# Maxima's row transfers from ACT's queue, setup work moved ahead, last adapter batch in halves

## The chip, the cores and the metric

The kernel runs on one core of one Trainium2 chip. The metric is the device time of one execution in microseconds. Five engines run their own instruction streams: TensorE (PE, with its weight loads as PEld), VectorE (DVE), ScalarE (ACT), GpSimd (POOL) and SyncE (SP). They wait for each other through semaphores. Transfers are issued by an engine (rows named SPq or ACTq) and run on the core's DMA engines.

## The reference

x is 4 x 512 x 256 (batches, tokens, features), float32. Four layers follow one another, each conditioned by a row per batch:

```
L0: x += g1 * (softmax(q k^T) v @ Wo + bo),  q, k, v from mod(ln(x)) @ W + b,  16 heads of 16
    x += g2 * (gelu(mod(ln(x)) @ W1 + b1) @ W2 + b2),  hidden 1024
L1: x += ga * (a state-space layer with 64 complex states over mod(ln(x)))
    x += gf * (gelu_tanh(mod(ln(x)) @ W1 + b1) @ W2 + b2)
L2: as L0, with rotary embedding of q and k and without most biases
L3: y = gelu(x @ a1 @ b1, rank 8) @ a2 @ b2,  a and b made from the condition row per batch
    out = x + y
```

## The kernel before

**Engine streams.** Each engine's program is written out: setup, attention 0 (`att0`), MLP 0, MLP 1 with the state-space layer, attention 1 (`att1`), MLP 2 with the low-rank adapter (`low`), and the adapter of the last batch at the very end. Everything on one engine runs in the written order.

**Attention.** A table, `attention_schedule`, gives every task a step number; each engine walks through the steps and does its own kinds of tasks. 16 steps make one group G of four heads of one batch, so there are 16 groups and 256 steps. Tasks with a step below LEAD = -34 are the lead, done before the loop. In a step n TensorE makes one score tile (line 636, one of 512 wide), one product for the running maxima (L645, 32 steps ahead; DVE reduces pairs of them in L819), and every fourth step the product with V (L666, PV). ACT takes the exponential of each score tile (L723) and, at step 16G+20, copies the group's result out (kind O, L684), after a wait for the last PV. ACT also copies T, Q and K (L694, L703, L706) out of PSUM.

**Banks.** The score tiles and the Q, K, V, T, M and PJ results rotate through three PSUM banks (7, 0, 1) in the order in which TensorE makes them. `open` makes TensorE wait until the former user of the bank has been read.

**Row maxima.** At step 16G-13 TensorE turns the maxima (M, L609), DVE negates them into a high and a low part (L780, L781), and at step 16G-12 the task MROW sends them as two extra rows of Q into the tiles of group G: four transfers within SBUF (L911), 4 KB each. At step 16G TensorE waits for them (`mset`). MROW is SP's task.

**Stores and fills.** q and k are split into a high and a low part (kinds SQ, SK), stored to DRAM (WQ, WK; `save_parts`, L883, three transfers each) and loaded again in another layout (FILL; `fill`, L893, four transfers per group). For batch 0 of att0 the order on SP is: stores of half 0, fill of group 0, stores of the second quarter, fill of group 1, stores of half 1, fills of groups 2 and 3, stores of batch 1, MROW of group 0. WK of half 0 alone is issued by ACT. TensorE waits for the fill of group g 32 steps before its first score tile.

**DVE in the start.** Statistics of batch 2 (LNS, L390, L397, L399) come at steps -24 to -12, and at step -12 DVE copies the turned modulation columns (`setup_turned_dve`) that TensorE turned at step -20 (`mod_turn`).

**The end.** For batch 3 the adapter runs alone: DVE adds the MLP's result to x (L1119, L1123), TensorE turns x (L430), DVE copies (L1541), down (L1547), copy (L1555), up (L1562), ACT's gelu (L1570), down (L1575), copy (L1583), up (L1590), DVE adds (L1597), SP stores (L1602).

Of the kernel before, what the change touches and what calls it, by code (L numbers as in the profile page):

```python
# [23 lines left out]
P = 128  # L24
B, T, D = 4, 512, 256
TT = T // P
# [36 lines left out]
def attention_schedule(rope):  # L63
# [6 lines left out]
    for b in range(B):  # L70
        o = 64 * (b - 1)
        first = b == 0
        for t in range(TT):
            put((-100, -84)[b] if b < 2 else o - 88 + 4 * t, "LNS", b, t)
        put((-99, -72)[b] if b < 2 else o - 75, "LNN", b, 0)
        for i in range(2):
            put((-90, -36)[b] + i if b < 2 else o - 65 + 2 * i, "T", b, i)
        for half in range(2):
            for k, c in enumerate("QK"):
# [7 lines left out]
                put((-67, -59)[half] if first else at + 14, "W" + c, b, half)  # L87
# [76 lines left out]
def build(nc, A, out):  # L164
    scheds = [attention_schedule(False), attention_schedule(True)]

    with ExitStack() as ctx:
# [336 lines left out]
        class Attention:  # L504
# [114 lines left out]
            def pe(self, pe):  # L619
# [3 lines left out]
                for n in self.steps(self.pe_task(pe)):  # L623
                    if n == LEAD and self.a:
                        pe.wait_ge(mlp1.acc_free, B)
                    elif n == -20 and self.a == 0:
                        mod_turn(pe, 2, 3, 6)
# [43 lines left out]
            def act_task(self, act):  # L671
                def task(kind, b, i):
                    if kind == "LNN" and self.a and b < 2:
                        norm_apply(act, "a1", b)
                    if self.a == 0 and (b, i) == (0, 0):
                        if kind == "WK":
                            self.save_parts(act, kind, b, i)
# [130 lines left out]
            def dve(self, v, link):  # L808
                for n in self.steps(self.dve_task(v, link)):
                    if n == -12 and self.a == 0:  # L810
# [84 lines left out]

            def sync_task(self, sp):
                def task(kind, b, i):
                    if kind in ("WQ", "WK"):
                        if kind == "WQ" or b or i or self.a:
# [6 lines left out]
                    elif kind == "MROW":  # L906
                        g = b % 4
                        self.wait_read(sp, "M", b, 0)
                        for r in range(2):
                            for c in range(2):  # L910
                                sp.dma_start(QD[g // 2][64 * r + SROWS + c:64 * r + SROWS + c + 1,  # L911
                                                        2 * (g % 2):2 * (g % 2) + 2, :].rearrange(
                                                            "p j (q c) -> p (j q) c", c=P),
                                             mneg_d[b % 2][8 - 8 * r:16 - 8 * r, c, :]).then_inc(self.mset[g], 16)
# [587 lines left out]
        class Low:  # L1502
# [95 lines left out]

            def sync(self, sp):
                for b in range(B):  # L1600
                    sp.wait_ge(f_oo, b + 1)
                    sp.dma_start(out[b].rearrange("(t p) d -> p t d", p=P), batch(b)).then_inc(out_done, 16)  # L1602
                sp.wait_ge(out_done, 16 * B)
# [377 lines left out]
        def mlp2_dve(v, link):  # L1981
# [27 lines left out]
            mlp2.dve_acc(v, 3)  # L2009
            low.dve_turned(v, 3)  # L2010
            low.dve_down(v, 3)
            low.dve_down2(v, 3)
            low.dve_out(v, 3)
# [4 lines left out]
        def _(pe):  # L2018
# [41 lines left out]
            pe.wait_ge(f_oo, 3)  # L2060
            low.turn(pe, 3)
            low.down(pe, 3)
            low.up(pe, 3)
            low.down2(pe, 3)
# [253 lines left out]
```

## Time and profile before

| | |
|---|---|
| three timed runs | 991.09 median, 979.3 to 994.69 us |
| profiled execution | 983.21 us, span 981.4 us |
| mean granted TensorE clock | 0.966 |
| busy: PE, DVE, ACT, POOL | 903.0, 586.9, 520.2, 417.5 us |
| att0, from its first exponential to its last O copy | 75.0 to 298.8 us |
| att1, the same | 617.6 to 842.4 us |

The span is the time from the first to the last instruction of one execution on the core. Busy times overlap between engines. A granted clock of 1.00 is TensorE's full speed, 0.50 half of it.

### The profile page before, as it was taken

To read this page: it belongs to the slowest core of one execution; us is meant where nothing else is said; L and a number is where in the kernel's file an instruction comes from. 1 tells how busy PE (TensorE), PEld (TensorE's weight loads), DVE (VectorE), ACT (ScalarE), POOL (GpSimd) and SP (SyncE) were. 2 spreads that over 40 slices of the span, in tenths; PEclk is the share of its full clock that TensorE was granted. 3 is DMA by queue.
4 is the path that set the end of the run, shared out by engine and by line. 5 is a ranking of instruction groups with operands and counts; after the bars stand their busy time and mean duration, and the time that the engine had idled before them with its cause. 6 is when DMAs were issued, how large, how long until landed. Compare 5 with 4: busy or idle time off the path is not lost.

```text
span 981.4 us, 14537 instructions
## 1 busy us (share of the span) xinstructions
PE 903.0 (92%) x5232; PEld 540.5 (55%) x5232; DVE 586.9 (60%) x911; ACT 520.2 (53%) x950; POOL 417.5 (43%) x556
## 2 busy tenths in 40 slices
PE   5769999899999889998999998899999999999995
PEld 3334444334336778786877774343443433687772
DVE  4565877688975375564433288478778884234223
ACT  2116777476766444345364432467677777644430
POOL 4241142242657545438545326462541116664330
PEclk9887999899999999999999999799999999999996
DMA  7366645545310230114114137365464421100001
GB/s 218 113 176 190 219 144 155 178 131 163 91 45 28 80 126 1 33 45 156 65 64 159 12 96 181 117 193 154 127 212 126 109 79 47 34 13 1 22 23 43
DMA packets 67135, 102.33 MB, mean 104 GB/s; under 512 B 16524, under 2 KB 27864, under 8 KB 66680
## 3 DMA queue, kind: packets, MB, share of 16 engines
q1 hardware_dynamic: 64804, 99.10, 33.5%
q10 hardware_dynamic: 2260, 2.30, 0.9%
q8 instruction: 42, 0.69, 0.3%
q14 instruction: 29, 0.24, 0.1%
HBM read 64.65 MB, written 36.07 MB: 103 GB/s over the span
## 4 chain that ended last, share of the span: by engine, by line
PE 70%; DVE 8%; DMA 5%; issue 5%; ACT 4%; SPq 4%; POOL 4%; ACTq 0%; DVEq 0%; POOLq 0%
PE PS L1042 11%; PE PS L666 11%; PE PS L636 11%; PE PS L1024 11%; PE PS L593 6%; PE PS L584 5%; PE PS L645 3%; ACT PH L723 2%; DMA d_parts<-UR 2%; PE PS L430 2%; DMA UR<-UR 2%; DVE U L819 2%; PE PS L604 2%; SPq L883 2%; PE PS L1157 1%
## 5 line engine op out<-in xcount | busy, mean ns | idle before, releaser
L819 DVE TENSOR_REDUCE U<-PS 128x2 f32<-128x1024 f32 x256 | 308.8, 1220 | 87.0 <-PE PS L645 85.8
L723 ACT ACTIVATE PH<-PS 128x512 f32<-128x512 f32 x512 | 277.6, 598 | 113.3 <-PE PS L636 110.0
L636 PE MATMUL PS<-UR 50*128 50x512 f32 x512 | 198.3, 458 | 23.2 <-DMA UR<-UR 15.1
L645 PE MATMUL PS<-UR 48*128 48x512 f32 x512 | 195.0, 475 | 14.1 <-DVE U L819 8.7
L636 PEld LDWEIGHTS PS<-UR 50*128 50x128 f32 x512 | 83.1, 188 | 180.0 <-ACT PH L723 105.3
L1089 POOL TENSOR_TENSOR PHR<-PH,PHR 128x512 fp32r<-128x512 f32 x96 | 128.8, 1347 | 119.7 <-ACT PHR L1079 119.7
L1042 PE MATMUL PS<-UR,PHR 128*128 128x256 f32 x768 | 158.7, 290 | 4.9 <-POOL PHR L1089 3.8
L666 PE MATMUL PS<-PH,U 128*32 128x512 f32 x1024 | 137.3, 609 | 0.0
L1042 PEld LDWEIGHTS PS<-UR,PHR 128*128 128x128 f32 x768 | 124.5, 189 | 22.5 <-issue 15.5
L1042 PE MATMUL PS<-W2R,PHR 128*128 128x256 f32 x384 | 108.2, 282 | 0.0
L1078 ACT ACTIVATE PH<-PS,col 128x512 f32<-128x512 f32 x64 | 43.9, 686 | 99.9 <-PE PS L1024 99.9
L645 PEld LDWEIGHTS PS<-UR 48*128 48x128 f32 x512 | 78.0, 189 | 31.2 <-DVE U L819 14.6
L1024 PE MATMUL PS<-UR 128*128 128x512 f32 x192 | 78.8, 411 | 4.7 <-issue 2.1
L584 PE MATMUL PS<-XN,WA 128*128 128x256 f32 x256 | 75.3, 428 | 2.2 <-ACT XN L694 2.2
L1024 PE MATMUL PS<-UR,W1R 128*128 128x512 f32 x192 | 76.7, 399 | 0.0
L1024 PE MATMUL PS<-XNR,UR 128*128 128x512 f32 x192 | 76.4, 398 | 0.0
L1042 PEld LDWEIGHTS PS<-W2R,PHR 128*128 128x128 f32 x384 | 72.3, 188 | 2.9 <-issue 1.2
L861 POOL TENSOR_TENSOR x<-x,tsc 128x256 f32<-128x256 f32 x32 | 23.5, 733 | 98.9 <-DVE tsc L792 98.2
L584 PEld LDWEIGHTS PS<-XN,WA 128*128 128x128 f32 x256 | 49.3, 207 | 22.9 <-issue 12.2
L404 POOL TENSOR_TENSOR rs<-ve,mhalf 128x4 f32<-128x4 f32 x24 | 25.2, 1051 | 76.9 <-DVE ve L399 76.7
L850 POOL TENSOR_TENSOR U<-U 128x512 f32<-128x512 f32 x16 | 20.4, 1277 | 65.6 <-issue 34.3
L1078 ACT ACTIVATE PH<-PS 128x512 f32<-128x512 f32 x32 | 19.1, 596 | 53.2 <-PE PS L1024 53.2
(221 smaller groups left out, 1251.9 us busy)
## 6 DMA issues: line engine op xcount, KB each, us to landing
UR<-d_parts SPq DMA_DIRECT2D x128, 192.0 KB, 4.1
d_parts<-UR SPq DMA_DIRECT2D x84, 256.0 KB
d_o<-U SPq DMA_DIRECT2D x32, 256.0 KB, 2.3
U<-in_L_cond_W_dram SPq DMA_DIRECT2D x8, 1024.0 KB, 7.7
W<-in_L_cond_W_dram SPq DMA_DIRECT2D x24, 256.0 KB, 3.0
U<-d_o SPq DMA_DIRECT2D x32, 128.0 KB
U<-d_rec SPq DMA_DIRECT2D x16, 256.0 KB
gates<-d_gate SPq DMA_DIRECT2D x3, 1024.0 KB, 5.2
```

What stands on the lines that cost most here:

```text
L404: link(pool.tensor_tensor(rs[:, 0, :], ve[:, :], mhalf[:, :], ALU.pow))
L584: ins = pe.matmul(dst[:, 0:D], WA[:, "QK".index(kind), k, h * P:(h + 1) * P], XN[:, b % 2, k, c], start=(k == 0), stop=(k == 1))
L593: ins = pe.matmul(dst[:, 0:D], src[:, k, i * P:(i + 1) * P], w[:, k, :], start=(k == 0), stop=(k == 1))
L636: self.close(pe.matmul(dst, KP[g // 2][r:r + SROWS + 2, j, kt * P:(kt + 1) * P], QP[g // 2][r:r + SROWS + 2, j, :], start=True, stop=True) ...
L645: ins = pe.matmul(bank(2 + (w + 2) % 4), QP[g // 2][r:r + SROWS, j, qt * P:(qt + 1) * P], KP[g // 2][r:r + SROWS, j, :], start=True, stop= ...
L666: ins = pe.matmul(PS[32 * j:32 * j + 32, 6, :], Vt[b % 2][:, kt, 4 * g + j, :], PH[:, m % 2, j, :], start=(kt == 0), stop=(kt == 3))
L723: nc.scalar.activation(PH[:, m % 2, j, :], self.where("ST", n), ACT.Exp).then_inc(self.a_free, 1)
L819: v.tensor_reduce(mx[:, G % 2, :].rearrange("p (r c) -> p r c", r=2)[:, :, c // 2], PS[:, 2 + (w + 1) % 4:4 + (w + 1) % 4, :], AX.X, ALU.m ...
L1024: ins = pe.matmul(bank(4 + q % 2), w[:, k, c], a[:, b % 2, k, :], start=(k == 0 and i == 0), stop=(k == 1 and i == 2))
L1042: ins = pe.matmul(self.acc(b, t), a[:, q % 4, c], w[:, m, :], start=(m == 0 and i == 0 and t % 2 == 0), stop=(m == FM - 1 and i == 2 and s ...
L1078: nc.scalar.activation(PH[:, 0, q % 4, :], bank(4 + q % 2), self.func, bias=bias)
L1089: pool.tensor_tensor(PHR[:, 0, q % 4, :], PH[:, 0, q % 4, :], HH[:, q % 4, :].bitcast(F32), ALU.subtract).then_inc(self.h_low, 1)
```

## The change

1. MROW of all groups of both attentions is ACT's task: `maxima(act, b)` waits for DVE's M result and issues the same four transfers from ACT's queue. SP issues none of them.
2. In att0, the stores of half 1 of batch 0 are issued by ACT at step -34, after group 0's fill has landed; SP keeps WQ of half 0 and the second quarter.
3. In att0, the statistics and the normalization of batch 2 are in the lead (steps -55 and -54); the evacuation of the modulation rows (`setup_more_dve`) is done ahead of the task FILL 2 in place of WQ 1; the turn and its columns come at the first step of the loop.
4. The adapter of batch 3 runs in halves of two token tiles, each with its own banks, copies and store; ACT and not DVE copies the turned x, and TensorE does two matmuls without use ahead of it.

```diff
--- before.py
+++ after.py
@@ -71,8 +71,8 @@
         o = 64 * (b - 1)
         first = b == 0
         for t in range(TT):
-            put((-100, -84)[b] if b < 2 else o - 88 + 4 * t, "LNS", b, t)
-        put((-99, -72)[b] if b < 2 else o - 75, "LNN", b, 0)
+            put((-100, -84)[b] if b < 2 else -55 if b == 2 and not rope else o - 88 + 4 * t, "LNS", b, t)
+        put((-99, -72)[b] if b < 2 else -54 if b == 2 and not rope else o - 75, "LNN", b, 0)
         for i in range(2):
             put((-90, -36)[b] + i if b < 2 else o - 65 + 2 * i, "T", b, i)
         for half in range(2):
@@ -84,7 +84,7 @@
                 if rope:
                     put(at + (1 if first else 5), "R" + c, b, half)
                 put(at + (2 if first else 7 if rope else 4), "S" + c, b, half)
-                put((-67, -59)[half] if first else at + 14, "W" + c, b, half)
+                put((-67, -59 if rope else -34)[half] if first else at + 14, "W" + c, b, half)
         for g in range(4):
             put((-62, -60, -57, -56)[g] if first else o + 17 + 16 * g, "FILL", b, g)
         for t in range(TT):
@@ -623,7 +623,7 @@
                 for n in self.steps(self.pe_task(pe)):
                     if n == LEAD and self.a:
                         pe.wait_ge(mlp1.acc_free, B)
-                    elif n == -20 and self.a == 0:
+                    elif n == LEAD:
                         mod_turn(pe, 2, 3, 6)
                     if n == 0:
                         pe.wait_ge(self.init, 1)
@@ -672,9 +672,13 @@
                 def task(kind, b, i):
                     if kind == "LNN" and self.a and b < 2:
                         norm_apply(act, "a1", b)
-                    if self.a == 0 and (b, i) == (0, 0):
-                        if kind == "WK":
-                            self.save_parts(act, kind, b, i)
+                    if kind == "WK" and self.a == 0 and b == 0:
+                        if i == 1:
+                            act.wait_ge(self.filled[0], FILLS)
+                            self.save_parts(act, "WQ", b, i)
+                        self.save_parts(act, kind, b, i)
+                    elif kind == "MROW":
+                        self.maxima(act, b)
                     if not self.on_act(kind) and kind != "O":
                         return
                     if kind == "O":
@@ -807,7 +811,7 @@
 
             def dve(self, v, link):
                 for n in self.steps(self.dve_task(v, link)):
-                    if n == -12 and self.a == 0:
+                    if n == LEAD and self.a == 0:
                         setup_turned_dve(v, link)
                     w = n + LOOK
                     if 0 <= w < NSTEP and w % 2:
@@ -893,25 +897,25 @@
                         sp.dma_start(dst[64 * r:64 * r + SROWS, 2 * (g % 2):2 * (g % 2) + 2, :],
                                      src[:, 4 * (g % 2) + r:4 * (g % 2) + 4:2, :]).then_inc(self.filled[g], 16)
 
+            def maxima(self, eng, G):
+                g = G % 4
+                self.wait_read(eng, "M", G, 0)
+                for r in range(2):
+                    for c in range(2):
+                        eng.dma_start(QD[g // 2][64 * r + SROWS + c:64 * r + SROWS + c + 1,
+                                                 2 * (g % 2):2 * (g % 2) + 2, :].rearrange("p j (q c) -> p (j q) c", c=P),
+                                      mneg_d[G % 2][8 - 8 * r:16 - 8 * r, c, :]).then_inc(self.mset[g], 16)
+
             def sync_task(self, sp):
                 def task(kind, b, i):
                     if kind in ("WQ", "WK"):
-                        if kind == "WQ" or b or i or self.a:
+                        if b or self.a or (kind, i) == ("WQ", 0):
                             self.save_parts(sp, kind, b, i)
                     elif kind == "FILL":
                         if (b, i) == (0, 1):
                             self.save_parts(sp, "WQ", 0, 0, 1)
                             self.save_parts(sp, "WK", 0, 0, 1)
                         self.fill(sp, b, i)
-                    elif kind == "MROW":
-                        g = b % 4
-                        self.wait_read(sp, "M", b, 0)
-                        for r in range(2):
-                            for c in range(2):
-                                sp.dma_start(QD[g // 2][64 * r + SROWS + c:64 * r + SROWS + c + 1,
-                                                        2 * (g % 2):2 * (g % 2) + 2, :].rearrange(
-                                                            "p j (q c) -> p (j q) c", c=P),
-                                             mneg_d[b % 2][8 - 8 * r:16 - 8 * r, c, :]).then_inc(self.mset[g], 16)
                     elif kind == "LDW":
                         if self.a and b == 0:
                             sp.wait_ge(mlp1.w2, FM * B)
@@ -1596,11 +1600,105 @@
                 xs = batch(b).rearrange("p (c a) d -> p a c d", a=2)
                 v.tensor_tensor(xs, xs, PS[:, 6:8, :].rearrange("p a (c d) -> p a c d", d=D), ALU.add).then_inc(f_oo, 1)
 
+            def last_pe(self, pe):
+
+                def half(c):
+                    return slice(D * c, D * (c + 1))
+
...
+                pe.wait_ge(f_oo, 3)
+                pe.wait_ge(mlp2.acc_free, B - 1)
+                for _ in range(2):
+                    pe.matmul(bank(5), WA[:, 0, 0, 0:P], WA[:, 1].rearrange("p k n -> p (k n)"), start=True, stop=True)
+                turn_half(0)
+                turn_half(1)
+                down_(0)
+                up_(0)
+                down_(1)
+                down2_(0)
+                up_(1)
+                up2_(0)
+                down2_(1)
+                up2_(1)
+
+            def last_act(self, act):
+                for c in range(2):
+                    act.wait_ge(f_t, 2 * B - 1 + c)
+                    nc.scalar.activation(xT[1][:, :, D * c:D * (c + 1)], bank(6 + c).rearrange("p (k n) -> p k n", k=DH),
+                                         ACT.Copy).then_inc(f_yo, 1)
+                for c in range(2):
+                    act.wait_ge(f_y, 2 * B - 1 + c)
+                    nc.scalar.activation(gT[1][:, :, D * c:D * (c + 1)], PS[:, 2 * c:2 * c + 2, 0:D],
+                                         ACT.Gelu).then_inc(f_yo, 1)
+
+            def last_dve(self, v):
+                b = B - 1
+                v.wait_ge(mlp2.w2, FM * B)
+                for c in range(2):
+                    v.tensor_tensor(tsc[:, 2 * c:2 * c + 2, :], bank(2 + c).rearrange("p (t d) -> p t d", d=D),
+                                    gates[:, 0, 1, b:b + 1, :].to_broadcast([P, 2, D]), ALU.mult).then_inc(mlp2.acc_free, 1)
+                    v.wait_ge(mlp2.acc_free, B + c)
+                    xs = x[:, TT * b + 2 * c:TT * b + 2 * c + 2, :]
+                    v.tensor_tensor(xs, xs, tsc[:, 2 * c:2 * c + 2, :], ALU.add).then_inc(mlp2.xd, 1)
+                for c in range(2):
+                    v.wait_ge(f_z, B + c)
+                    v.tensor_copy(z1[1][:, D * c:D * (c + 1)], bank(4 + c, D)).then_inc(f_zo, 1)
+                for c in range(2):
+                    v.wait_ge(f_z2, B + c)
+                    v.tensor_copy(z2[1][:, D * c:D * (c + 1)], bank(4 + c, D)).then_inc(f_z2o, 1)
+                for c in range(2):
+                    v.wait_ge(f_o, B + c)
+                    v.wait_ge(mlp2.xd, B + c)
+                    xs = x[:, TT * b + 2 * c:TT * b + 2 * c + 2, :]
+                    v.tensor_tensor(xs, xs, PS[:, 6 - 6 * c:8 - 6 * c, 0:D], ALU.add).then_inc(f_oo, 1)
+
             def sync(self, sp):
-                for b in range(B):
+                for b in range(B - 1):
                     sp.wait_ge(f_oo, b + 1)
                     sp.dma_start(out[b].rearrange("(t p) d -> p t d", p=P), batch(b)).then_inc(out_done, 16)
-                sp.wait_ge(out_done, 16 * B)
+                for c in range(2):
+                    sp.wait_ge(f_oo, B + c)
+                    t = slice(2 * c, 2 * c + 2)
+                    sp.dma_start(out[B - 1].rearrange("(t p) d -> p t d", p=P)[:, t, :],
+                                 batch(B - 1)[:, t, :]).then_inc(out_done, 16)
+                sp.wait_ge(out_done, 16 * (B + 1))
 
 
         att0, att1 = Attention(0, 6), None
@@ -2006,11 +2104,7 @@
             low.dve_down(v, 2)
             low.dve_down2(v, 2)
             low.dve_out(v, 2)
-            mlp2.dve_acc(v, 3)
-            low.dve_turned(v, 3)
-            low.dve_down(v, 3)
-            low.dve_down2(v, 3)
-            low.dve_out(v, 3)
+            low.last_dve(v)
 
         block = ctx.enter_context(nc.Block())
 
@@ -2057,12 +2151,7 @@
                     mlp2.product1(pe, q + 2)
                 mlp2_pe(pe, q)
                 mlp2.product2(pe, q)
-            pe.wait_ge(f_oo, 3)
-            low.turn(pe, 3)
-            low.down(pe, 3)
-            low.up(pe, 3)
-            low.down2(pe, 3)
-            low.up2(pe, 3)
+            low.last_pe(pe)
 
         @block.scalar
         def _(act):
@@ -2115,7 +2204,7 @@
                 if q < 3:
                     mlp2.act_w2(act, q + 1)
             low.act_gelu(act, 2)
-            low.act_gelu(act, 3)
+            low.last_act(act)
 
         @block.vector
         def _(v):
@@ -2134,7 +2223,7 @@
             v.tensor_copy(czero2[:, :], czero[:, :]).then_inc(mods_set, 1)
             setup_columns(v, link)
             for t in lead[turned_:]:
-                if t == ("WQ", 0, 1):
+                if t == ("FILL", 0, 2):
                     setup_more_dve(v, link)
                 att0.dve_task(v, link)(*t)
             att0.dve(v, link)
```

Left out above are the helpers of `last_pe`: each does one piece of `low` (turn, down, up, down2, up2) for 256 of the 512 tokens, waiting for its own half's copy.

## Rows read from the trace of the kernel before

**Rows 1.** The page, busy time of each engine.

```profile
PE 903.0 (92%) x5232; PEld 540.5 (55%) x5232; DVE 586.9 (60%) x911; ACT 520.2 (53%) x950; POOL 417.5 (43%) x556
```

**Rows 2.** Timeline of all engines, 107 to 126: start, us, engine, line, what.

```profile
109.90 3.74 SPq L911 DMA_DIRECT2D UR<-UR  x4
...
110.79 0.60 ACT L684 ACTIVATE U<-PS 128x512 f32<-128x512 f32 x1 [0.43 <-PE PS L666]
...
111.29 1.08 ACT L723 ACTIVATE PH<-PS 128x512 f32<-128x512 f32 x2
...
112.38 0.50 PE L636 MATMUL PS<-UR 50*128 50x512 f32 x1
...
125.21 0.50 PE L636 MATMUL PS<-UR 50*128 50x512 f32 x1 [0.17 <-ACT PH L723]
```

**Rows 3.** Line 911 alone: ns min/median/max of one issue.

```profile
L911 SPq DMA_DIRECT2D UR<-UR x128: 620/656/1797, 66.3 to 819.3; - x128
```

**Rows 4.** Timeline of ACT, 0 to 31.

```profile
3.12 0.21 ACT L1355 ACTIVATE csig<-col 128x8 f32<-128x8 f32 x1 [0.17 <-DVE col L1367]
3.13 0.37 ACTq L2074 DMA_DIRECT2D WA<-in_L_cond_Wq_dram  x1
3.54 0.49 ACTq L2074 DMA_DIRECT2D WA<-in_L_cond_Wk_dram  x1
...
24.80 3.25 ACTq L883 DMA_DIRECT2D d_parts<-UR  x3
28.09 0.84 ACT L703 ACTIVATE U<-PS,col 128x256 f32<-128x256 f32 x2 [3.49 <-issue]
```

**Rows 5.** Timeline of SP, around 354, the later load of the same kind.

```profile
354.42 0.47 SPq L2236 DMA_DIRECT2D WA<-in_L_cond_Wk_dram  x1
```

**Rows 6.** Timeline of PE, instructions after long idle times (in brackets).

```profile
60.39 0.50 PE L645 MATMUL PS<-UR 48*128 48x512 f32 x2 [2.48 <-DVE U L819]
...
74.23 0.76 PE L636 MATMUL PS<-UR 50*128 50x512 f32 x1 [6.56 <-DMA UR<-UR]
...
179.79 0.50 PE L636 MATMUL PS<-UR 50*128 50x512 f32 x1 [3.61 <-DMA UR<-UR]
...
300.25 0.74 PE L1024 MATMUL PS<-UR 128*128 128x512 f32 x1 [2.08 <-issue]
...
331.77 0.39 PE L1042 MATMUL PS<-UR,PHR 128*128 128x256 f32 x1 [2.50 <-POOL PHR L1089]
...
476.37 0.50 PE L1024 MATMUL PS<-UR 128*128 128x512 f32 x1 [1.94 <-DVE XNR L1111]
...
616.80 0.76 PE L636 MATMUL PS<-UR 50*128 50x512 f32 x1 [4.99 <-DMA UR<-UR]
```

**Rows 7.** Busy time by stretch; the granted clock stands before DMA share and GB/s.

```profile
61.30:64.70 3.40, 3.40 (x11) 2.21 (x10) 1.96 (x3) 0.47 (x1) 3.31 (x4) 0.51 0.90 197
75.00:84.80 9.80, 9.56 (x28) 5.09 (x27) 4.14 (x5) 5.28 (x10) 0.34 (x1) 0.50 0.69 238
300.70:303.60 2.90, 2.90 (x8) 2.23 (x7) 1.51 (x8) 0.44 (x1) 1.56 (x2) 0.50 0.10 23
332.00:335.00 3.00, 3.00 (x20) 2.60 (x20) 0.00 (x0) 0.66 (x2) 2.59 (x8) 1.00 0.26 72
477.90:481.10 3.20, 3.20 (x12) 2.79 (x11) 1.34 (x8) 1.26 (x2) 1.75 (x6) 0.50 0.00 0
...
965.00:969.00 4.00, 2.40 (x11) 0.57 (x12) 1.46 (x3) 0.00 (x0) 0.00 (x0) 0.50 0.00 0
```

**Rows 8.** Timeline of all engines, the end: the turn and the last store.

```profile
963.16 1.94 PE L430 MATMUL PS<-ident,x 128*128 128x128 f32 x8 [2.67 <-DVE x L1123]
...
978.06 0.37 SPq L1602 DMA_DIRECT2D out_dram<-x  x1
```

**Rows 9.** Timelines of DVE and SP, the first maxima.

```profile
55.25 0.28 DVE L781 SCALAR_TENSOR_TENSOR UR<-PS,UR 16x128 fp32r<-16x128 f32 x1
...
66.28 3.20 SPq L911 DMA_DIRECT2D UR<-UR  x4
```

More of the change, by code:

```diff
@@ L1597, in dve_out, with turn_half, down_half, down_ @@
                 v.tensor_tensor(xs, xs, PS[:, 6:8, :].rearrange("p a (c d) -> p a c d", d=D), ALU.add).then_inc(f_oo, 1)
+            def last_pe(self, pe):
+                def half(c):
+                    return slice(D * c, D * (c + 1))
+                def turn_half(c):
+                    pe.wait_ge(mlp2.xd, B + c)
+                    for k in range(DH):
+                        for t in range(2):
+                            ins = pe.transpose(PS[:, 6 + c, D * k + P * t:D * k + P * (t + 1)],
+                                               x[:, TT * (B - 1) + 2 * c + t, k * P:(k + 1) * P], ident[:, :])
+                    ins.then_inc(f_t, 1)
+                def down_half(j, src, c):
+                    for g in range(4):
+                        ins = pe.matmul(PS[32 * g:32 * g + 32, 4 + c, 0:D], wide[:, j, B - 1, g % 2, :],
+                                        src[1][:, g % 2, half(c)], start=True, stop=True)
+                    return ins
+                def down_(c):
+                    pe.wait_ge(f_yo, 2 * B - 1 + c)
+                    down_half(0, xT, c).then_inc(f_z, 1)
+                def up_(c):
+                    pe.wait_ge(f_zo, B + c)
+                    for h in range(DH):
+                        r = slice(64 * h, 64 * h + 64)
+                        ins = pe.matmul(bank(2 * c + h, D), btr[r, 0, B - 1, h * P:(h + 1) * P], z1[1][r, half(c)],
+                                        start=True, stop=True)
+                    ins.then_inc(f_y, 1)
+                def down2_(c):
+                    pe.wait_ge(f_yo, 2 * B + 1 + c)
+                    down_half(2, gT, c).then_inc(f_z2, 1)
+                def up2_(c):
+                    pe.wait_ge(f_z2o, B + c)
+                    for t in range(2):
+                        r = slice(64 * t, 64 * t + 64)
+                        ins = pe.matmul(bank(6 - 6 * c + t, D), z2[1][r, (2 * c + t) * P:(2 * c + t + 1) * P],
+                                        btr[r, 1, B - 1, :], start=True, stop=True)
+                    ins.then_inc(f_o, 1)
+                pe.wait_ge(f_oo, 3)
[12 more added lines that the diff above has]
+                up2_(1)
```

## The prediction

> **What bounds the kernel now.** I read the page first. TensorE is busy for 92% of the span and ACT for 53% [rows 1], so the kernel is a TensorE stream with some holes, and a change pays either by closing a hole or by opening one. Then I listed every TensorE idle time above 0.9 us. Four of these holes lie where the change works [rows 6]: 2.48 us ended by a DVE reduction at 60.39, and 6.56 us at 74.23, 3.61 us at 179.79 and 4.99 us at 616.80, these three ended by the maxima's row transfers (UR<-UR). After the longest the granted clock is 0.50, the 1.2 GHz level, from 75 to 84.8 [rows 7].
>
> Why the first of these row transfers is late is seen in two rows: its data were ready at 55.53, when DVE ended L781, but SP issued it at 66.28 [rows 9], because SP goes through its tasks in order and fills and stores stood ahead of it.
>
> The steady loop of one group, 16 steps, comes next (223.8 us of att0's table entry over 16 groups are 14.0), since 30 of 32 of the moved tasks fall into it. In the timeline of a group with a V product every fourth step [rows 2] the reader should see how little ACT runs behind TensorE: ACT's O copy starts at 110.79, the exponentials of steps 4 and 5 follow at 111.29, in 1.08 us, and TensorE's L636 of step 6, which needs the first of them, starts at 112.38. Score tiles, V, Q, K and M share three PSUM banks, so a score product waits for the exponential of its third predecessor in the rotation. Where no such product lies between, ACT is the last to come: TensorE's L636 at 125.21 waits 0.17 us for it [rows 2]. ACT has 47% idle time over the span, but in lumps of some half microsecond; it has none of several microseconds that TensorE doesn't feel.
>
> **The change, part by part.**
>
> *The maxima's transfers on ACT's queue.* One issue costs SP 656 ns at the median and 620 at the least [rows 3]; four come to 4 x 0.656 + 3 x 0.04 = 2.74 us. The trace has no such transfer on ACT, so its cost there is bounded. The nearest pair is the same load of a 256 KB weight: 0.37 (Wq) and 0.49 us (Wk) on ACT [rows 4], 0.47 (Wk) on SP [rows 5]. An issue costs the same on both, and I take 2.74 us. The low end is 4 x 0.37 + 0.12 = 1.6 us, as for that cheapest load on ACT; the high end is the stores on ACT, 3.25 us for three [rows 4], or 4.3 for four.
>
> Does ACT compute meanwhile? After the three stores at 24.80 the next activation starts at 28.09, and its idle time of 3.49 us is put down to issue [rows 4]. So the issue holds ACT up. But the activation ahead overlaps: L2074 starts at 3.13, 0.01 us after the activation ahead of it [rows 4]. At a group's MROW (step 4) the instruction ahead is the O copy of an earlier group. The M result is there by then (SP issued at 109.90 [rows 2], before the O copy at 110.79), so the added wait itself costs nothing. The four issues run from 110.80 to 113.54. Queued behind them are the exponentials of steps 4 to 7 and the Q or K copies, and TensorE waits for those. Step 4's exponential would start at 113.54 and not at 111.29, 2.25 us later. The following L636 has at most 112.38 less 111.83 (111.29 + 0.54), or 0.55 us, of slack, some of it the semaphore's way; I take 0.35 to 0.45. That leaves a hole of 1.8 us in groups with a product every fourth step, and 2.2 us where ACT already is the last to come. ACT then catches up within the next steps, but TensorE, the bound, doesn't. Mean 2.0 us. G = 0 of either attention has no exponentials behind it, so 2 x 15 = 30 groups pay: **+60 us**, with ends of 30 x 0.9 = 27 and 30 x 3.6 = 108 (a hole is the issue time less some 0.7 us, so 1.6 less 0.7 and 4.3 less 0.7).
>
> The Trainium skill speaks against this edit (DMA: Bandwidth & Descriptors, section "Issuing engines are not separate DMA queues"): transfers begun from several engines run on the same DMA engines, and only the sequencer's time for the issue is saved, "usually small relative to the DMA itself". Here that issue time is the whole matter, and it moves from SP, which waits for others most of the time, to the engine nearest to the bound. By that page alone the sum would stay near nought.
>
> *The clock.* A hole has a second price. Of the holes between 1.9 and 2.5 us [rows 6], those at 60.39 (2.48), 300.25 (2.08) and 476.37 (1.94) were followed by a stretch at 0.50, the one at 331.77 (2.50) was not [rows 7]; eight shorter ones (1.0 to 1.6 us, not shown) were not either. Such a stretch is 2.9 to 3.4 us long [rows 7] and costs half of that, 1.7 us. The new holes are at the lower edge of this: from none to 3 in 4 of 30 may drop the clock. I take 12: **+20 us**, ends 0 and 23 x 1.7 = 39.
>
> *The three waits for the row transfers.* ACT is free when M is ready for G = 0, so the transfer goes at 55.5 and not at 66.3 [rows 9]. It took 74.23 less 69.48 (66.28 + 3.20), 4.75 us, from the last issue to TensorE's start, so it lands near 63, and TensorE reaches step 0 at 67.67 less the 4 us of the next part, near 64. The wait of 6.56 us goes, and with it the 9.8 us at half clock behind it, of which I count 4.0 us as won and the rest as latency. What is late next are the fills of group 2. They need the half-1 stores, which leave ACT as soon as group 0's fill has landed and no longer SP after group 1's fill; they land earlier, so the fills do too. ACT has hardly other work there, and three banks cover its Q copies if they come some 4 us later. If these six stores crowd the quarter-1 stores beside them, group 1's fill could be 1 to 2 us late. Attention 1: 4.99 us and 3.3 us for its slow stretch (some 7 us). G = 6 of attention 0: 3.61 us and, by the same share, 2.4. Sum **-10.6 - 8.3 - 6.0 = -25 us**.
>
> *Statistics of batch 2, modulation turn and columns into the lead.* DVE and TensorE wait there for group 0's fill, so they are covered. This takes away what stood before 60.39: 2.48 us and the slow stretch behind it, 1.7 [rows 7]: **-4 us**. PE's four transposes fall before group 0's fill, at no cost.
>
> *The last batch's adapter in halves.* Now the chain from the turn at 963.16 to the last store's issue at 978.06 [rows 8] is 14.9 us of nine dependent pieces, at clock 0.50 (965 to 969 [rows 7]). In halves, the residual of half 0 is ready 1.2 us earlier, and half 0's pieces run under half 1's. TensorE's ten half pieces take 1.0 us each at clock 0.50 (a whole turn took 1.94) and 0.5 at full clock, and DVE's and ACT's copies 0.4 to 0.7 each. Placed one behind the other in the new order, the last issue comes at 970.6 if the two added matmuls keep the clock up, and at 974.4 if not: 4 to 8 us less, taken as **-6 us**.
>
> *SP without MROW* and the moved gate loads change nothing: nobody waits for SP after these edits.
>
> **The sum.** -25 - 4 - 6 = -35, +60 + 20 = +80, net +45 us. The profiled execution took 983.2 us (span 981.4), 8 us less than the median of the three timed runs, 991.1, which lie between 979.3 and 994.7. I count from 987, the mean of the two: **1032 us**.
>
> **Rivals.**
> *The issues are hidden (ends on the other side).* Place: ACT's queue at step 4 of each group. If the sequencer got to the four issues while earlier exponentials are still queued in the engine, only a part would delay step 4's. Against it: L2074 had no wait of its own, yet went only at 3.13, with the activation ahead (3.12) that had waited for DVE [rows 4]; so an issue doesn't pass a waiting instruction. It decides from 35 / 30 = 1.2 us of hole per group, that is issues of 1.9 us in all. Fully hidden: 987 - 35 = 952. Half hidden (a hole of 1.0 us, no clock drops): 952 + 30 = 982. The Trainium skill gives ScalarE an instruction queue 8 deep in strict order (TensorE: Matmul & The Clock Gate, "Architectural detail: the array is 16× 32×32, not 1× 128×128"); by that rule it would be the fully hidden case, and the row at 3.13 speaks against it.
> *The holes come, the clock holds.* For: none of the eight shorter holes dropped it. 952 + 60 = 1012.
> *The clock drops after nearly every hole.* For: three of four did. 952 + 60 + 51 = 1063.
> *The start doesn't shorten as told.* The half-1 stores on ACT crowd the fills and the start keeps its 15 us: 1032 + 15 = 1047.
>
> **How the numbers follow.** Forecast (holes, some drops; 1015 to 1048) 0.42; clock holds 0.20; drops nearly always 0.10; start kept 0.11; half hidden 0.11; fully hidden 0.06. 8 in 10 go from 1000 to 1063: that leaves out both hidden cases (0.17) and a bit at the top. A measurement of this kernel can tell about 2%, 20 us, from no change. Faster than 971: 0.06. Within 971 to 1011: half hidden and a third of the case at 1012, 0.18. Slower: 0.76.
>
> **What would show it.** ACTq rows for the maxima of 0.62 to 0.70 us each beside ACT's O copy; after them TensorE holes of 1.8 to 2.2 us, ended by ACT's L723 line; O copies 16 us apart where they were 14.0; TensorE's mean clock below 0.966 and stretches of 0.50 in the attentions. No wait for UR<-UR at step 0. The forecast is wrong if ACT's issues take under 0.4 us, or if O copies stay 14 us apart.

## The result, and the profile after

The changed kernel takes **1097.9 us** at the median of four runs (1093.2 to 1099.6), the one before 985.9: a ratio of 1.115, with an interval of 1.105 to 1.125. It is 112 us slower, where +45 was forecast. The profiled executions span 1097.1 us and 981.4 us. Where the runs of one kernel fell into a fast state and a slow one, over 1.5% longer (experiments 2, 4, 8 and 12), the median given is that of the fast ones alone.

From the page of the kernel after: its busy times, the granted clock by slices, the chain, and the costliest group of TensorE. The line numbers have moved by a few: L636 is still the score product, the exponential is L727, the O copy L688, the row transfers L905.

```profile
PE 974.3 (89%) x5256; PEld 560.7 (51%) x5256; DVE 588.3 (54%) x914; ACT 522.0 (48%) x952; POOL 416.3 (38%) x556
...
PEclk9788888887889999999999997897979688799999
...
PE 71%; ACT 7%; ACTq 7%; DVE 5%; issue 4%; POOL 3%; DMA 3%; SPq 1%; DVEq 0%; POOLq 0%
...
L636 PE MATMUL PS<-UR 50*128 50x512 f32 x512 | 229.8, 526 | 74.8 <-ACT PH L727 73.4
```

Against [rows 1], DVE, ACT and POOL are busy for nearly the same time. TensorE, with 24 matmuls more, is busy for 71 us more. Work didn't grow: the same 512 score products take 526 ns each, where they took 458 before, and TensorE stood idle ahead of them for 73.4 us, waiting for exponentials (L727). On the chain of work that ended last, ACT's transfer issues (ACTq) have 7% of the span, where they had none. The clock's digits (tenths of full speed in 40 slices) show where TensorE was slower: mostly 8 in attention 0, 6 to 9 in attention 1, 9 between and behind them. So two things are to be told apart, idle time and slower matmuls.

I cut both executions at the first and the last score product of each attention. The windows (columns: stretch, its length, busy time of PE, PEld, DVE, ACT, POOL, granted clock, DMA share, GB/s) of the kernel before:

```profile
0.00:74.23 74.23, 48.58 (x168) 28.23 (x168) 40.49 (x92) 12.63 (x23) 29.81 (x47) 0.91 0.57 168
74.23:296.10 221.87, 210.55 (x1205) 87.79 (x1206) 172.41 (x237) 154.00 (x289) 81.14 (x155) 0.96 0.49 146
296.10:616.80 320.70, 297.64 (x1739) 235.75 (x1738) 165.50 (x312) 141.69 (x241) 167.62 (x210) 0.99 0.26 82
616.80:839.70 222.90, 216.20 (x1225) 89.01 (x1228) 161.61 (x194) 158.34 (x301) 78.91 (x82) 0.98 0.44 127
839.70:981.40 141.70, 130.03 (x906) 99.74 (x904) 46.85 (x78) 53.53 (x98) 59.99 (x64) 0.93 0.06 21
```

and of the kernel after:

```profile
0.00:71.38 71.38, 52.74 (x169) 30.92 (x169) 39.11 (x91) 11.87 (x23) 27.35 (x46) 0.83 0.60 180
71.38:353.40 282.02, 238.98 (x1208) 94.86 (x1210) 174.76 (x239) 155.45 (x290) 82.77 (x157) 0.84 0.39 114
353.40:667.20 313.80, 295.98 (x1738) 234.45 (x1735) 164.17 (x310) 139.67 (x240) 163.64 (x207) 0.99 0.26 80
667.20:963.10 295.90, 258.60 (x1226) 101.12 (x1226) 163.99 (x195) 160.20 (x303) 82.45 (x86) 0.82 0.35 99
963.10:1097.10 134.00, 128.00 (x930) 99.38 (x928) 46.23 (x81) 54.85 (x100) 60.04 (x64) 1.00 0.07 22
```

By stage the change gives -2.8, **+60.1**, -6.9, **+73.0** and -7.7 us, together +115.7. The loss lies in the two loops of 16 groups; every other stage gained.

One group of the kernel after, in the timeline:

```profile
211.43 0.60 ACT L688 ACTIVATE U<-PS 128x512 f32<-128x512 f32 x1 [0.43 <-PE PS L666]
211.43 2.62 ACTq L905 DMA_DIRECT2D UR<-UR  x4
...
214.15 2.27 ACT L727 ACTIVATE PH<-PS 128x512 f32<-128x512 f32 x4 [2.13 <-DVE tsc L796]
...
214.80 0.50 PE L636 MATMUL PS<-UR 50*128 50x512 f32 x1 [1.71 <-ACT PH L727]
...
215.72 1.82 PE L666 MATMUL PS<-PH,U 128*32 128x512 f32 x8
...
220.68 1.07 PE L666 MATMUL PS<-PH,U 128*32 128x512 f32 x8
```

ACT spends 2.62 us on the four issues; the next exponential follows at 214.15 (the releaser named there, L796, is not what held it: ACT's own queue is). TensorE has used up its three banks and waits 1.71 us. The product behind it, L666 at 215.72, takes 1.82 us where its like at 220.68 takes 1.07: the clock has fallen (0.50 from 216 to 219) and comes back in between. The O copies of attention 0 are 17.3 us apart on average (15 intervals from 95.95 to 355.41). Measured the same way they were 13.4 apart before (96.77 to 298.23); the forecast put this at 14.0 before and 16 after. Slow stretches can be longer, as windows some groups later show:

```profile
252.00:263.00 11.00, 9.49 (x53) 3.40 (x45) 8.21 (x10) 5.45 (x11) 1.28 (x1) 0.93 0.46 110
264.60:273.40 8.80, 8.80 (x34) 3.07 (x32) 4.10 (x4) 2.82 (x6) 0.00 (x0) 0.50 0.34 134
276.00:283.00 7.00, 6.23 (x37) 2.57 (x29) 5.97 (x9) 3.41 (x7) 0.85 (x2) 1.00 0.62 151
285.00:293.00 8.00, 8.00 (x30) 2.57 (x28) 4.10 (x4) 2.94 (x6) 2.15 (x4) 0.50 0.14 51
```

The stretch from 264.6 to 273.4 is wholly at the 1.2 GHz level with TensorE busy all the time. Read so in steps of 1 us, the clock is at 0.5 in 26 stretches of the two loops, about 192 us in all or 7.4 each; in the loops of the kernel before it was in 3, 26 us in all. One of the 26 stands at the start of attention 1, as one did before; the other 25 follow 25 of the 29 holes of over 1.4 us that TensorE waited for exponentials. The four holes with no slow stretch behind them were 1.55, 1.72, 2.26 and 2.67 us long, and the shortest with one was 1.50, so length alone doesn't tell them apart.

### The profile page after: what moved, and what is told of

It reads as the page before. It is cut to its first block, busy times and chain, and to the rows that moved or that the text cites. A ratio compares the mean times of both kernels' runs of the same rounds, so it can differ in the third digit from the quotient of the medians.

```text
span 1097.1 us, 14588 instructions
## 1 busy us (share of the span) xinstructions
PE 974.3 (89%) x5256; PEld 560.7 (51%) x5256; DVE 588.3 (54%) x914; ACT 522.0 (48%) x952; POOL 416.3 (38%) x556
## 4 chain that ended last, share of the span: by engine, by line
PE 71%; ACT 7%; ACTq 7%; DVE 5%; issue 4%; POOL 3%; DMA 3%; SPq 1%; DVEq 0%; POOLq 0%
PE PS L666 14%; PE PS L636 13%; PE PS L1046 10%; PE PS L1028 9%; ACTq L905 6%; PE PS L593 6%; PE PS L584 5%; PE PS L645 4%; ACT PH L727 4%; PE PS L604 2%; PE PS L430 2%; DMA d_parts<-UR 2%; ACT U L688 2%; PE PS L1161 1%; PE PS L1149 1%
## 5 line engine op out<-in xcount | busy, mean ns | idle before, releaser
L727 ACT ACTIVATE PH<-PS 128x512 f32<-128x512 f32 x512 | 277.9, 598 | 228.5 <-PE PS L636 151.5
L636 PE MATMUL PS<-UR 50*128 50x512 f32 x512 | 229.8, 526 | 74.8 <-ACT PH L727 73.4
L636 PEld LDWEIGHTS PS<-UR 50*128 50x128 f32 x512 | 97.5, 217 | 274.3 <-ACT PH L727 162.9
L645 PE MATMUL PS<-UR 48*128 48x512 f32 x512 | 224.0, 537 | 9.3 <-DMA UR<-d_parts 6.5
L666 PE MATMUL PS<-PH,U 128*32 128x512 f32 x1024 | 166.9, 730 | 0.0
L645 PEld LDWEIGHTS PS<-UR 48*128 48x128 f32 x512 | 92.7, 218 | 23.4 <-issue 9.1
L584 PE MATMUL PS<-XN,WA 128*128 128x256 f32 x256 | 80.8, 452 | 4.2 <-ACT XN L698 4.2
L584 PEld LDWEIGHTS PS<-XN,WA 128*128 128x128 f32 x256 | 52.5, 221 | 27.4 <-issue 15.2
L593 PE MATMUL PS<-WA,XN 128*128 128x256 f32 x128 | 44.6, 480 | 1.1 <-ACT U L707 1.1
L666 PEld LDWEIGHTS PS<-PH,U 128*32 128x32 f32 x1024 | 21.5, 116 | 44.8 <-issue 16.7
```

Source lines behind the costliest of these rows:

```text
L584: ins = pe.matmul(dst[:, 0:D], WA[:, "QK".index(kind), k, h * P:(h + 1) * P], XN[:, b % 2, k, c], start=(k == 0), stop=(k == 1))
L593: ins = pe.matmul(dst[:, 0:D], src[:, k, i * P:(i + 1) * P], w[:, k, :], start=(k == 0), stop=(k == 1))
L636: self.close(pe.matmul(dst, KP[g // 2][r:r + SROWS + 2, j, kt * P:(kt + 1) * P], QP[g // 2][r:r + SROWS + 2, j, :], start=True, stop=True) ...
L645: ins = pe.matmul(bank(2 + (w + 2) % 4), QP[g // 2][r:r + SROWS, j, qt * P:(qt + 1) * P], KP[g // 2][r:r + SROWS, j, :], start=True, stop= ...
L666: ins = pe.matmul(PS[32 * j:32 * j + 32, 6, :], Vt[b % 2][:, kt, 4 * g + j, :], PH[:, m % 2, j, :], start=(kt == 0), stop=(kt == 3))
L727: nc.scalar.activation(PH[:, m % 2, j, :], self.where("ST", n), ACT.Exp).then_inc(self.a_free, 1)
```

## The experiments

Times are medians; the kernel before, timed beside each batch of experiments, was between 984.7 and 987.6. I held three theories. **A**: the issues on ACT open a hole in every group, and the clock falls after nearly each; both cost. **B**: the issues alone are the price and the clock is a symptom. **C**: another part of the change costs.

**1. All row transfers back on SP**, the rest kept.

```diff
 # act_task
-                    elif kind == "MROW":
-                        self.maxima(act, b)
 # sync_task
+                    elif kind == "MROW":
+                        self.maxima(sp, b)
```

> The changed kernel with the row transfers of the maxima on SP's queue in every group again; half-1 stores on ACT, statistics and the halved last adapter stay. Theory A (nearly the whole loss is the issue time on ACT and the TensorE clock that it costs): the 1097.9 us fall by the two loops' loss of 59.8 + 72.7 = 132 us, to about 965 to 985. Theory C (the stores on ACT, the statistics or the adapter cost a part): it stays 20 us or more above 985, over 1005.

Measured 970.7 us, ratio 0.984 (0.977 to 0.991; a ratio is to the kernel before). The windows of its two loops:

```profile
71.71:291.07 219.36, 208.49 (x1208) 86.31 (x1210) 173.66 (x239) 154.44 (x290) 82.88 (x157) 0.97 0.49 147
611.11:835.14 224.03, 216.11 (x1225) 89.04 (x1229) 161.80 (x194) 158.35 (x301) 78.94 (x82) 0.98 0.44 126
```

The loops are as long as before the change, to 3 us. The rest of the change is a small gain, and C falls.

**2. Only the row transfers moved**, in the kernel before (its MROW branch leaves `sync_task`; `act_task` calls `maxima(act, b)`).

> The kernel before with one part of the change alone: the row transfers of all 32 groups begun from ACT's queue. Theory A: it carries the whole loss, 985 + 112 to 132 less the some 15 us that the earlier first step of either attention gives: 1085 to 1110. Theory C: clearly less, under 1060. The forecast on record, with its holes of 2.0 us and 12 drops, would give 60 + 20 - 25 = +55, 1040.

Measured 1091.3 us, of two runs that lie apart (1083.4 and 1099.2), ratio 1.105 (1.091 to 1.119): this one part carries the whole loss, to within what these runs can tell. In the profile (1099.2 us) the loops are 277.8 and 295.7 us; the start is 6.0 us shorter, and the stretch between the attentions 6.7 us.

**3. On ACT for the first group of either attention alone.**

```diff
-                    elif kind == "MROW":
+                    elif kind == "MROW" and b == 0:
                         self.maxima(act, b)
 # sync_task
+                    elif kind == "MROW" and not (b == 0):
+                        self.maxima(sp, b)
```

> The changed kernel with the row transfers on ACT for the first group of either attention alone and on SP for the other 30. Theory A: no holes inside the loops, and both starts are shortened as they were: 965 to 975, under the run with all on SP by what the first wait for the rows costs (up to 10.6 and 8.3 us). Rival: SP's queue is free by then at either start since the half-1 stores left it, and this run and the one with all on SP agree within 3 us.

Measured 968.7 us, ratio 0.982 (0.975 to 0.989). Against experiment 1 that is 2 us, less than the two intervals can tell, so both the forecast and its rival stand by the time. The profiles show that each was right for one attention. The stretch between the attentions is 314.0 us against 320.0: ahead of attention 1, TensorE waited 4.62 us for the rows with all on SP, and doesn't here. In attention 0 neither kernel has such a wait at step 0, since SP's queue is free without the half-1 stores; start and loop together are 293.5 against 291.1, no gain.

**4. The holes filled.** The last S product ahead of the hole is repeated eight times into the same bank, before its signal; the result is the same.

```diff
-                        ins = pe.matmul(bank(2 + (w + 2) % 4), ...)
+                        for _ in range(9 if n % 16 == 5 else 1):
+                            ins = pe.matmul(bank(2 + (w + 2) % 4), ...)
```

(the dummy product of the last steps likewise)

> The changed kernel, its transfers on ACT in all groups, with 8 repeats of one 0.21 us S product on TensorE in the step ahead of each hole (1.7 us of matmuls that repeat a result), so that TensorE is busy while ACT issues. The exponentials wait as long as before. Theory A (hole and clock multiply): the clock stays at 1.0 in the loops, the slow stretches go (TensorE's busy time had grown by 28 us in the first loop and 42 us in the second), and the time falls by 40 to 70 us to 1030 to 1060. Theory B (the issues on ACT are the whole price, the clock is a symptom beside it): within 10 us of 1098.

Measured 1042.6 us, ratio 1.053 (1.044 to 1.062): 55.3 us less than the changed kernel, although TensorE does 288 matmuls more. Its timeline around one group, and the windows of its two loops:

```profile
214.41 2.62 ACTq L907 DMA_DIRECT2D UR<-UR  x4
...
214.85 1.98 PE L646 MATMUL PS<-UR 48*128 48x512 f32 x9
...
217.78 0.50 PE L636 MATMUL PS<-UR 50*128 50x512 f32 x1 [0.72 <-ACT PH L729]
...
218.21 1.06 PE L668 MATMUL PS<-PH,U 128*32 128x512 f32 x8
```

```profile
73.70:324.50 250.80, 236.77 (x1336) 108.98 (x1337) 175.29 (x239) 154.95 (x290) 83.55 (x158) 0.98 0.43 127
...
638.80:898.10 259.30, 246.17 (x1354) 111.57 (x1356) 164.50 (x195) 159.91 (x303) 82.77 (x86) 0.98 0.39 113
```

(L646 is the S product here, L668 PV.) ACT issues as long, 2.62 us, and releases TensorE as late; but TensorE has worked until 0.72 us before, the clock stays at 0.98, and L668 takes 1.06 us. B falls. This splits the price: filled holes against none (experiment 1) 71.9 us, idle against filled holes 55.3 us. By the profiles' loops it is 66.7 and 67.8 us. The 29 holes of the changed kernel sum to 69.3 us, so the first part is about what the holes alone explain. Read in steps of 1 us, the loops here are at 0.5 for about 20 us, against 192: a microsecond at half clock cost 0.3 to 0.4 us, not a half.

**5, 6 and 12. One, two and three of each group's four on ACT**, the others on SP. Both engines call `maxima`; `on_act` is true in ACT's call and false in SP's.

```diff
+                        if (2 * r + c < 1) == on_act:   # 2 in experiment 6, 3 in experiment 12
                             eng.dma_start(QD[g // 2][...], mneg_d[G % 2][...]).then_inc(self.mset[g], 16)
```

> The changed kernel with one of each group's four row transfers on ACT and three on SP, in all groups. Theory A (the burst on ACT opens a hole of its length less the half to one us that the score banks cover, 2.4 us for four issues of 2.6, and each such hole costs 1.8 us more by the clock): one issue of 0.65 us lies under the cover, no holes, no drops: 965 to 975, as with all on SP. Rival (every issue on ACT costs its length): 30 x 0.65 = 20 us more, 990.

> The changed kernel with two of each group's four row transfers on ACT and two on SP. Theory A: 1.3 us of issues less 0.5 to 1.0 of cover leave holes of 0.3 to 0.8 us in 30 groups, 9 to 24 us, too short for the clock to fall: 980 to 995. Rival (the clock already falls after short holes): 2 us each more, over 1020. By proportion of the whole loss of 127 us: 1034.

> The changed kernel with three of each group's four row transfers on ACT and one on SP. Two on ACT left holes of 1.07 us and the clock up, four left 1.7 to 2.4 and the clock down after nearly each. By length three leave 1.07 + 0.66 = 1.7 us: 30 x 1.7 = 51 us, 1022, if the clock stays up; with half of the drops 1045; with the clock down after each, at 1.9 us, 1078. Theory A takes 1040 to 1078; a price in proportion to the issues on ACT would be 970.7 + 3/4 x 127 = 1066 (two gave 17 of 127 where proportion had 64, so it is already unlikely).

Measured 968.5 us (ratio 0.980, 0.974 to 0.986), 987.4 us (1.000, 0.997 to 1.004) and 1038.4 us (1.053, 1.045 to 1.061). With the ends of the series, none and four, and with the granted clock, the median over the same runs:

| on ACT | us | over none | mean clock |
|---|---|---|---|
| 0 | 970.7 | | 0.971 |
| 1 | 968.5 | -2.2 | 0.975 |
| 2 | 987.4 | +16.7 | 0.976 |
| 3 | 1038.4 | +67.7 | 0.941 |
| 4 | 1097.9 | +127.2 | 0.900 |

A price per issue would be a straight line, and one of burst length alone a straight line behind the first. The step from two to three is 51 us, 30 x 0.66 = 20 of them by length, and it is there that the clock begins to fall. Three came out just under theory A's 1040 to 1078, nearest to its case of half of the drops (1045). Two fell into theory A's range, though with longer holes than its 0.3 to 0.8 us. Experiment 6 shows a hole, and the window around it:

```profile
122.57 0.49 PE L636 MATMUL PS<-UR 50*128 50x512 f32 x1 [1.08 <-ACT PH L727]
```

```profile
80.00:200.00 120.00, 111.05 (x648) 46.08 (x644) 89.56 (x106) 83.16 (x156) 39.72 (x62) 1.00 0.57 172
```

Eight holes of 0.38 to 1.27 us, each ended by an exponential, lie in these 120 us, and the mean clock is 1.00 over them. With three on ACT the holes of the first loop are 1.04 to 2.56 us (in the profile, an execution of 1048.4 us, longer than the median), with four 1.55 to 4.08.

**7. All four on ACT in every fourth group only** (`b % 4 == 2`, 8 groups in all).

> The changed kernel with all four row transfers on ACT in every fourth group only (groups 2, 6, 10, 14 of either attention, 8 in all) and on SP in the others: the price of a hole that stands alone. If each costs what 30 of them cost on average, (1097.9 - 970.7) / 30 = 4.2 us: 970.7 + 34 = 1005. If holes apart from each other cost what the forecast took, 2.0 us and 1.7 in 12 of 30 cases: 970.7 + 8 x 2.7 = 992. If the clock never falls after a lone one: 970.7 + 8 x 2.4 = 990.

Measured 1009.3 us, ratio 1.020 (1.013 to 1.027): 38.6 us over experiment 1, **4.8 us for each hole**. They need no neighbours to be dear. The eight are 2.28 to 4.21 us long, 2.7 at the mean, and seven of them are followed by a slow stretch; the shortest, at 665.41, isn't. Two of them, a stretch behind each, and two stretches away from any:

```profile
162.80 0.79 PE L636 MATMUL PS<-UR 50*128 50x512 f32 x1 [3.40 <-ACT PH L727]
...
276.29 0.79 PE L636 MATMUL PS<-UR 50*128 50x512 f32 x1 [2.42 <-ACT PH L727]
```

```profile
150.00:160.00 10.00, 9.40 (x57) 4.00 (x49) 7.66 (x9) 6.30 (x12) 2.31 (x2) 1.00 0.55 138
163.00:173.00 10.00, 10.00 (x36) 3.45 (x36) 3.68 (x3) 4.46 (x10) 2.31 (x2) 0.50 0.36 100
180.00:218.00 38.00, 36.87 (x223) 15.04 (x221) 32.16 (x39) 27.19 (x51) 15.45 (x44) 1.00 0.57 159
277.00:291.00 14.00, 13.99 (x59) 4.22 (x57) 6.50 (x7) 7.04 (x14) 8.17 (x12) 0.50 0.11 31
```

**8. All four on ACT in all groups, one at a time.**

```diff
-        put(16 * G - 12, "MROW", G, 0)
+        for i in range(4):
+            put(16 * G - (12, 10, 7, 5)[i], "MROW", G, i)
```

> The changed kernel with all four row transfers of every group on ACT, but begun one at a time, 12, 10, 7 and 5 steps ahead of the group's first score in place of all at 12. ACT issues as long in all (32 x 2.6 us) but never more than 0.65 us between two exponentials. Theory A (the burst is the price): the holes are gone, 965 to 980. Rival (ACT's total time is the price, as it is 70% busy in the loops and the copies of queries and keys fall in the same steps): a part of the 127 us stays, over 1000.

Measured 973.0 us, ratio 0.985 (0.977 to 0.993). It is all but experiment 1's time: 125 of the 127 us are gone, and the other 2 are less than these runs can tell. ACT still issues all 128 transfers, most in 0.63 us each, now between exponentials (L728):

```profile
207.66 0.63 ACTq L907 DMA_DIRECT2D UR<-UR  x1
208.38 0.60 ACT L728 ACTIVATE PH<-PS 128x512 f32<-128x512 f32 x1
208.44 0.63 ACTq L907 DMA_DIRECT2D UR<-UR  x1
208.88 1.57 ACT L728 ACTIVATE PH<-PS 128x512 f32<-128x512 f32 x3
```

It was the burst, not ACT's load. The schedule has a weak point: the last row goes out only five steps ahead, and in the trace it lands late now and then, at the worst by this:

```profile
102.21 0.79 PE L637 MATMUL PS<-UR 50*128 50x512 f32 x1 [2.37 <-DMA UR<-UR]
```

**9 to 11. The other parts**, each undone in the kernel of experiment 3: the half-1 stores on SP (`-34` to `-59`, the ACT branch for them out), the last adapter whole (the calls of `last_pe`, `last_act`, `last_dve` back to `low`'s), the statistics of batch 2 and the modulation turn and columns in their old steps.

> The kernel with rows on ACT for the first group alone (968.7 us), and its half-1 stores of the start begun from SP again, in their old places. Theory A (a burst of issues on ACT costs there too): six stores held ACT for 9.7 us at the start, and TensorE waited 2.1 us for the copies of queries and keys behind them; step 0 comes earlier than 70.3, by some 2 us, as in the kernel before with only the rows moved (68.3): 964 to 968. Rival (the forecast on record: the stores on ACT land earlier and shorten the start): 3 to 6 us later, 972 to 975.

> The kernel with rows on ACT for the first group alone (968.7 us), and the last adapter whole as before. The forecast on record gave the halves 6 us: 974.7; the tail should be 20.9 us long again against 14.1, with the TensorE clock at 0.5. Rival: the output's transfer hides it, within 2 us of 968.7.

> The kernel with rows on ACT for the first group alone (968.7 us), and the statistics of the third batch element, and the turn and columns of the modulation, in their old places inside the loops. The forecast on record gave their move 4 us: 972 to 973. Rival: they lie beside other work in either place, within 2 us, or they delay the start and cost it.

Measured 971.0, 976.6 and 970.0 us, ratios 0.985 (0.980 to 0.989), 0.990 (0.986 to 0.994) and 0.984 (0.978 to 0.990), against 968.7 and 0.982 of experiment 3. The adapter's halves give 7.9 us, and every run with the whole adapter is over every run of experiment 3 (971.2 at the least against 970.4 at the most); in the profile the part behind attention 1's last product is 141.1 us with the whole adapter and 134.0 with halves. The other two are under what these runs can tell. The stores are the more instructive: on SP, step 0 comes at 62.5 and not at 70.2, but the loop behind it is 235.4 us long and not 223.3. TensorE waits there for what SP then sends late:

```profile
65.11 0.49 PE L645 MATMUL PS<-UR 48*128 48x512 f32 x1 [2.21 <-DMA UR<-d_parts]
...
87.20 0.79 PE L636 MATMUL PS<-UR 50*128 50x512 f32 x1 [3.80 <-DMA UR<-UR]
```

So theory A's forecast for it (964 to 968) missed: the earlier start is real and given back. The statistics look alike in the profiles: with them in their old places step 0 comes at 77.2 and not at 70.2, and the loop is 218.2 us long and not 223.3.

## Why the prediction was too low

The direction was right, and so was the mechanism of the hole: ACT's issues open one in 29 groups of the forecast's 30, it is about 1.7 or 2.4 us long in most where 1.8 and 2.2 were forecast, and the O copies stand further apart. The sum failed by 67 us, most of it in one step.

- **The clock, +20: the step that failed.** "From none to 3 in 4 of 30 may drop the clock. I take 12", at 1.7 us each. It fell behind 25 of 29 holes, and the stretches were 7.4 us long, not 2.9 to 3.4. Experiment 4 puts the price at 55 to 68 us, over the stated end of 39. Three of four holes of such length had been followed by 0.50 [rows 7]; I discounted them by eight shorter ones, and took the length of the slow stretch from the two MLP stages and the start, though the one row of a loop, 75 to 84.8, was 9.8 us long [rows 7], and my own term for attention 1 counted a stretch of "some 7 us". The rival "drops nearly always" had the count nearly right, but at 1.7 us each it also stopped at 1063. Half of 7.4 us would have been too much in turn: by experiment 4 a drop cost some 2.1 to 2.7 us. Experiment 7 shows that density isn't the reason: a hole with three groups of none between it and the next costs 4.8 us, against 2.0 + 0.7 in the forecast. Why the clock fell behind some holes and not behind others, and what ended a slow stretch, stays open.
- **The holes, +60.** Mis-sized by 7 to 12 us: experiments 4 and 1 differ by 66.7 us in the loops and 71.9 at the medians. Fifteen holes of attention 0 sum to 37.8 us and fourteen of attention 1 to 31.5. Most of the excess sits in six groups with holes of 2.9 us and more, where the four issues took longer than 2.74 us. Two of them, the issues and the hole behind:

```profile
75.73 4.98 ACTq L905 DMA_DIRECT2D UR<-UR  x4
...
81.41 0.79 PE L636 MATMUL PS<-UR 50*128 50x512 f32 x1 [4.08 <-ACT PH L727]
...
171.71 4.61 ACTq L905 DMA_DIRECT2D UR<-UR  x4
...
177.07 0.79 PE L636 MATMUL PS<-UR 50*128 50x512 f32 x1 [3.71 <-ACT PH L727]
```

  The median issue on ACT is 0.63 us, 0.66 on SP, so "an issue costs the same on both" held, but the median hid the long ones, 1797 ns already on SP [rows 3] and up to 2626 ns on ACT. The end of 4.3 us held all but three of the bursts.
- **The three waits, -25.** Too large. Attention 1's gave 6 to 7 us (8.3 forecast; experiments 2 and 3). The start gave 6.0 with the rows alone and 2.8 in the changed kernel (10.6 forecast). ACT's six half-1 stores took 10.73 us on its queue and held back the copies of queries and keys, and group 1's fill came later; the rows of the kernel after:

```profile
39.17 10.73 ACTq L887 DMA_DIRECT2D d_parts<-UR  x6
...
50.53 2.07 PE L593 MATMUL PS<-WA,XN 128*128 128x256 f32 x4 [1.08 <-ACT U L707]
...
57.66 0.79 PE L645 MATMUL PS<-UR 48*128 48x512 f32 x2 [2.63 <-DMA UR<-d_parts]
```

  Three banks were to cover ACT's Q copies "if they come some 4 us later"; they came behind the whole 10.73 us of issues, and TensorE waited 1.08 us for them. That the stores there shorten the start was false: by experiment 9 they move a wait from the loop to the start. The wait of 3.6 us at group 6 did go, and it is still there (2.72 us) in experiment 1.
- **Statistics -4 and last adapter -6.** Measured 1.3 at the medians (3.2 in the profiles), not to be told from nought, and 7.9 (7.1 in the profile). The clock stayed up there, as hoped for:

```profile
1083.76 1.88 PE L1649 MATMUL PS<-WA 128*128 128x512 f32 x4
...
1093.65 1.27 SPq L1699 DMA_DIRECT2D out_dram<-x  x2
```

- **The base of 987** held (985.9). With what was measured the sum is: holes +67 to +72, clock +55 to +68, waits about -13 (2.8 + 6.9 + 3.6), statistics -1 to -3, adapter -7 to -8, or +98 to +119, around the measured +112.
- **The rivals.** The issues were not hidden, and the rows at 211.43 and 214.15 show how it goes: the first issue starts with the O copy and doesn't wait for its end, but the next exponential waits for all four. By the Trainium skill ScalarE has an instruction queue in strict order (TensorE: Matmul & The Clock Gate, "Architectural detail: the array is 16× 32×32, not 1× 128×128"). The trace agrees with the order, and it doesn't lead to the fully hidden case that the prediction drew from it: the queue let the issues begin early here, by the 0.60 us of the O copy, and no more. The Trainium skill calls the issue time "usually small relative to the DMA itself" (DMA: Bandwidth & Descriptors, "Issuing engines are not separate DMA queues"). For this change that doesn't carry over: bursts of 2.6 us and more on the engine that feeds the bound cost 4.2 us per group, holes and clock together, where the same issues on SP opened none of these holes.

## What to carry to other kernels

A queue's place is priced by the burst, not by its sum: 128 issues on ACT cost 127 us in bursts of four and, one at a time, no more than these runs can tell from nought. So spread issues over the steps, or leave them on the engine that is waited for least. Price a TensorE hole with its clock, by a slow stretch of the same stage, and take the drop as the rule once rows at that length show it in most cases. Where only one transfer of a class is late, try moving that one: the first group's alone took 6 us off the stretch ahead of attention 1 in the profile, though the whole gain of 2 us over all on SP isn't shown by the times.

## What the hardware showed beyond that

- A slow stretch can go on while TensorE is busy all the time: 8.8 us at 0.50 with 8.80 us of busy time, and 14 us after a 2.42 us hole in experiment 7. At 0.5 the loop's exponentials come every 3.1 us per two steps (267.33, 270.48, 273.50 in the kernel after), at full clock every 1.7 us (275.45, 277.12, 278.85).
- Repeating a matmul in a hole, which does nothing useful, took 55 us off a kernel whose TensorE is its bound.
- The same four issues on ACT take 2.60 to 2.64 us in most groups and up to 5.0 us in others; six stores there took 10.73 us, 1.8 us each. What sets this wasn't tried.
